# An audio tower's Mamba loop on one Trainium2 core: the order of each engine's work in a loop step is redrawn

## What is computed

```python
h = tok(x)                                   # (64, 128, 256)
xz = layernorm(h) @ W_in                     # 256 -> 2 x 512
xc = silu(conv4(x_inner) + conv_b)           # causal, along the positions
delta_raw, Bm, Cm = split(xc @ W_xproj)      # 1, 16, 16 columns
delta = softplus(delta_raw * w_dt + b_dt)
state = exp(delta * A) * state + delta * Bm * xc      # 16 states for each of 512 channels
y = (sum over states of state * Cm + xc * D) * silu(z)
h = h + y @ W_out
h = h + moe(layernorm(h))                    # softmax, top 2 of 8, silu(x@wg) * (x@wi) @ wo
```

## Time and profile before

| | |
|---|---|
| median of 3 runs | 3155.86 us (3154.88 to 3156.69) |
| profiled execution, its own time | 3151.46 us |
| its span | 3149.5 us |
| busy: PE, DVE, ACT, POOL | 85%, 69%, 47%, 55% |
| Mamba loop (first scan of step 0 to first idle after step 15) | about 120 to 2290 us |
| tail and table, then experts | 2290 to 2341 us, then to the end |
| mean granted TensorE clock | 0.94 of 2.4 GHz |

### The profile page before, as it was taken

The page is one execution under the profiler, slowest core; times in us unless marked ns, Lnnn a source line. Parts: engine busy times, 40 slices in busy tenths (PEclk is TensorE's granted clock), DMA queues, the critical chain, the costliest instruction groups (busy, mean ns, idle before and its releaser), DMA issues. The chain is left out here.

```text
span 3149.5 us, 32678 instructions
## 1 busy us (share of the span) xinstructions
PE 2668.0 (85%) x7774; PEld 1311.5 (42%) x7775; DVE 2170.9 (69%) x2417; ACT 1475.8 (47%) x2717; POOL 1722.5 (55%) x816
## 2 busy tenths in 40 slices
PE   3588897887978788797878879788659999999999
PEld 1234343333434333343433334343236666666665
DVE  0499898988989889898988989899932222222222
ACT  1565556466565646655564665556312222222222
POOL 1467667576766757676675767667522222222222
PEclk9899898999989899998989998898879999999999
DMA  1321304132140413213040321303152222222221
GB/s 37 122 84 50 135 13 140 41 113 104 42 137 10 140 40 114 104 42 135 12 140 30 123 104 42 134 11 136 36 194 45 46 42 45 43 45 45 43 46 30
DMA packets 125600, 235.91 MB, mean 75 GB/s; under 512 B 46449, under 2 KB 93714, under 8 KB 109122
## 3 DMA queue, kind: packets, MB, share of 16 engines
q1 hardware_dynamic: 99378, 200.65, 19.3%
q0 software_dynamic: 26128, 34.36, 6.3%
HBM read 182.22 MB, written 53.78 MB: 75 GB/s over the span
## 5 line engine op out<-in xcount | busy, mean ns | idle before, releaser
L531 POOL TENSOR_TENSOR arena<-u,arena 128x2048 f32<-128x2048 f32 x256 | 1158.3, 4527 | 468.8 <-DVE psum L898 464.0
L1216 PE MATMUL psum<-hc,ident 128*128 128x512 f32 x2048 | 1094.9, 662 | 340.2 <-DVE hc L906 339.5
L898 DVE TENSOR_TENSOR_SCAN psum<-psum,arena 128x1024 f32<-128x1024 f32 x512 | 1172.4, 2290 | 135.7 <-ACT psum L709 112.4
L1216 PEld LDWEIGHTS psum<-hc,ident 128*128 128x128 f32 x2048 | 390.4, 205 | 893.7 <-DVE hc L906 546.5
L709 ACT ACTIVATE psum<-delta,a_neg 128x508 f32<-128x508 f32 x1024 | 656.5, 674 | 0.6
L906 DVE TENSOR_TENSOR hc<-psum,arena 128x1024 f32<-128x1024 f32 x512 | 626.2, 1223 | 15.5
L595 POOL DMA_INDIRECT out_dram<-hres,tok_id x136 | 211.6, 1556 | 598.6 <-ACT hres L835 549.5
L1348 PE MATMUL psum<-arena,xnt 128*128 x1088 | 515.6, 596 | 0.0
L1108 DVE COPY z<-psum 128x512 f32<-128x512 f32 x136 | 94.1, 692 | 461.3 <-PE psum L1357 461.3
L835 ACT ACTIVATE hres<-psum,tok_w 128x256 f32<-128x256 f32 x136 | 64.5, 474 | 454.4 <-PE psum L1367 447.7
L1367 PE MATMUL psum<-arena,z 128*128 x1088 | 257.1, 379 | 0.9 <-DVE z L1108 0.9
(11 more groups left out here) (147 smaller groups left out, 1961.8 us busy)
## 6 DMA issues: line engine op xcount, KB each, us to landing
arena<-ssm_rows SPq DMA_DIRECT2D x128, 1024.0 KB, 6.1
delta<-expert_rows SPq DMA_DIRECT2D x136, 129.0 KB, 2.1
h_saved_rows<-hnew SPq DMA_DIRECT2D x16, 512.0 KB, 6.6
hres<-h_saved_rows SPq DMA_DIRECT2D x16, 512.0 KB, 4.2
out_dram<-h SPq DMA_DIRECT2D x16, 512.0 KB, 3.0
draw<-ssm_rows SPq DMA_DIRECT2D x16, 256.0 KB, 4.0
arena<-in_L_ffn_wg_dram SPq DMA_DIRECT2D x8, 512.0 KB, 9.9
arena<-in_L_ffn_wi_dram SPq DMA_DIRECT2D x8, 512.0 KB, 10.0
```

What stands on the lines that cost most here:

```text
L531: pool.tensor_tensor(dBx[k % 2], rep, b_rep[:, q * QN:(q + 1) * QN, :], ALU.mult).then_inc(dbx_ready, 1)
L898: nc.vector.tensor_tensor_scan(h, h, src, 0.0, ALU.mult, ALU.add).then_inc(scan_done, 1)
L1216: last = nc.tensor.matmul(yacc, ident[:, :], hc[k % 2][:, i, :], start=False, stop=(k % HC == HC - 1 and i == 1))
```

## The change

Nothing is computed otherwise; places in the lists move, and two buffers with them.

- VectorE: `gate_y` of a chunk stands one half unit later (k = 9, 17, 25, and 1 of the next step, before: 8, 16, 24, 0). `residual` at 6 and 8 (5 and 9), `stats2` at 10 (9), `stats1` at 18 (30), `router_a` at 26 (19), `router_b` cut in three at 27, 28, 29 (all at 21), `router_c` at 31 (24).
- TensorE: `project_z` at 0 to 3 (0, 1, 4, 5), `project_out` at 4 to 7 (2, 3, 6, 7), `turn_xn` at 6, 7 (8, 9), `project_x` and `conv` from 8 to 19 (10 to 21), `x_ssm` at 21 (23), `turn_x` at 12, 13 and `embed` at 14, 15 (25 to 28), `turn_row` at 23, 24 (15, 16), `router` at 25 (18), `count` at 30 (22). `skip` stays at 0, 8, 16, 24.
- ScalarE: its copies follow these; `norm1` at 4 (3), `silu_x` at 20 (22), `norm2` at 21, 22 (12, 13), softplus at 25 to 29 and 31 (26 to 29 and 31).
- GpSimd: both sets of scatters of group g - 2 in step g, in units 2, 3, 6, 7 (before: the first set in step g - 1, units 13, 14; the second in step g, units 1, 2); `rsqrt` for the second normalization in unit 8 (6); that for the first, now of group g + 2, in unit 11 (1). Those of group 1 come before the loop.
- SyncE: `save_h` ahead of `share_ssm`.
- `xt` lies in `yz` and no longer in `h2`; both results of `embed` use `bank_b`.

```diff
-        xt = [h2[0:KX, 2 * m:2 * m + 2, :].rearrange("p b c -> p (b c)") for m in range(2)]
+        xt = [yz[0:KX, 2 + m, :] for m in range(2)]
-        emb_bank = [bank_a, bank_b]
+        emb_bank = [bank_b, bank_b]
 # SyncE, step
+                if more:
+                    save_h(g + 2)
                 if not last:
                     share_ssm(g + 1)
-                if more:
-                    save_h(g + 2)
...
 # GpSimd, step and tail
+                    if not second:
+                        if k in (2, 3):
+                            scatter(g - 2, 0, 2 * (k - 2))
+                        if k == 5:
+                            second_weight(g - 2)
+                        if k in (6, 7):
+                            scatter(g - 2, 1, 2 * (k - 6))
+                    if k == 8 and not first:
                         rsqrt(g - 1, 1, stat2, pow2)
+                    if k == 11 and more:
+                        rsqrt(g + 2, 0, stat1, pow1)
...
+            def tail(g):
+                both_scatters(g - 1)
+                rsqrt(g, 1, stat2, pow2)
+                both_scatters(g)
...
 # ScalarE, step (its new places)
+                    if k < NCH:
+                        evac_z(g, k)
+                        if k == 4:
+                            norm1(g + 1)
+                        if k in (6, 7):
+                            evac_xnt(g + 1, k - 6)
+                        if k in (8, 11, 14, 17):
+                            evac_xi(g + 1, (k - 8) // 3)
                         if k in (10, 13, 16, 19):
+                            evac_conv(g + 1, 1 - par, (k - 10) // 3)
+                        if k == 20:
+                            silu_x(g + 1, 1 - par)
...
 # VectorE, step
-                    if k == 0 and not first:
+                    if k == 1 and not first:
                         gate_y(g - 1, NCH - 1)
-                    if k > 0 and k % HC == 0:
+                    if k > 1 and k % HC == 1:
                         gate_y(g, k // HC - 1)
                     times_c(g, k)
...
 # TensorE, step
-                    if k in (0, 1, 4, 5):
-                        project_z(g, {0: 0, 1: 1, 4: 2, 5: 3}[k], not last)
-                    if k in (2, 3, 6, 7) and not first:
-                        project_out(g - 1, k // 4, k % 2, more)
+                    if k < NCH:
+                        project_z(g, k)
+                    if k in (4, 5, 6, 7) and not first:
+                        project_out(g - 1, (k - 4) // 2, k % 2)
                     if not last:
+                        if k in (6, 7):
+                            turn_xn(g + 1, k - 6)
+                        if k in (8, 11, 14, 17):
+                            project_x(g + 1, (k - 8) // 3)
+                        if k in (9, 12, 15, 18):
+                            conv(g + 1, (k - 9) // 3, 0)
                         if k in (10, 13, 16, 19):
+                            conv(g + 1, (k - 10) // 3, 1)
+                        if k == 21:
                             x_ssm(g + 1, 1 - par)
+                    if more:
+                        if k in (12, 13):
+                            turn_x(g + 2, k - 12)
+                        if k in (14, 15):
+                            embed(g + 2, k - 14)
                     if not first:
+                        if k in (23, 24):
+                            turn_row(g - 1, k - 23, more)
+                        if k == 25:
                             router(g - 1)
+                        if k == 30:
                             count(g - 1)
```

More of the change, by code:

```diff
@@ L561, in step, with both_scatters @@
                         make_u(g, par, c)
[L562 to L568, removed]
-                        rsqrt(g - 1, 1, stat2, pow2)
[L570 to L577, removed]
+                    if not second:
[6 more added lines that the diff above has]
+                    if k == 8 and not first:
+                        rsqrt(g - 1, 1, stat2, pow2)
+                    if k == 11 and more:
+                        rsqrt(g + 2, 0, stat1, pow1)
+            def both_scatters(g):
                 scatter(g, 0, 0)
@@ L788, in step @@
[L788 to L798, removed]
@@ L799, in step @@
-                    if k == 29 and not last:
-                        softplus_relu(g + 1, 1)
-                        softplus_relu(g + 1, 2)
+                        if k == 25:
+                            softplus_abs(g + 1)
+                        if k == 26:
+                            softplus_exp(g + 1)
+                        if k == 27:
+                            softplus_ln(g + 1)
+                            softplus_relu(g + 1, 0)
+                        if k in (28, 29):
+                            softplus_relu(g + 1, k - 27)
@@ L938, in router_a, with router_b @@
                 nc.vector.tensor_tensor(ex[:, :, :], logits, bc(lmax[:, :]), ALU.subtract).then_inc(lsub_ready, 1)
-            def router_b(g):
-                dve.wait_ge(lexp_ready, g + 1)
-                nc.vector.tensor_reduce(esum[:, :], r_ex, AX_X, ALU.add).then_inc(dv, 1)
-                after(g, 2)
-                nc.vector.reciprocal(einv[:, :], esum[:, :]).then_inc(dv, 1)
-                after(g, 3)
-                nc.vector.tensor_tensor(r_gates, r_ex, bc(einv[:, :]), ALU.mult).then_inc(dv, 1)
-                n = 4
-                ahead(dve, second_set, g)
-                for k, src in ((0, r_gates), (1, r_g2)):
+            def router_b(g, part):
+                if part == 0:
+                    dve.wait_ge(lexp_ready, g + 1)
+                    nc.vector.tensor_reduce(esum[:, :], r_ex, AX_X, ALU.add).then_inc(dv, 1)
+                    after(g, 2)
+                    nc.vector.reciprocal(einv[:, :], esum[:, :]).then_inc(dv, 1)
+                    after(g, 3)
+                    nc.vector.tensor_tensor(r_gates, r_ex, bc(einv[:, :]), ALU.mult).then_inc(dv, 1)
+                    ahead(dve, second_set, g)
+                if part in (1, 2):
+                    k, src, n = ((0, r_gates, 4), (1, r_g2, 10))[part - 1]
                     after(g, n)
@@ L1045, in tail @@
                 router_a(g)
-                router_b(g)
+                for part in range(3):
+                    router_b(g, part)
                 router_c(g)
@@ L1141, in turn_x @@
                     ahead(pe, emb_free, 2 * g)
-                    ahead(pe, slot_ready, g - 2)
+                    ahead(pe, h2_ready, 2 * (g - 2))
                 else:
@@ L1323, in tail @@
                     for b in range(2):
-                        project_out(g, m, b, False)
-                turn_row(g, 0)
-                turn_row(g, 1)
+                        project_out(g, m, b)
+                turn_row(g, 0, False)
+                turn_row(g, 1, False)
                 router(g)
```

113 lines of the change are left out of this document (43 added, 70 removed).

## The result

The changed kernel takes 3239.69 us (median of 4 runs, 3237.93 to 3242.37) against 3155.37 us (4 runs, 3152.49 to 3156.69): ratio 1.0268, 95% interval 1.0253 to 1.0283, 84 us slower. The direction was forecast; the time lies 18 us above the top of the range. The profiled execution has a span of 3236.8 us at a mean granted clock of 0.938, against 3149.5 and 0.939: the clock as a whole has not changed. One of the four runs of the kernel of experiment 3 took 6392.02 us, the others 3103.68 to 3111.43; its ratio is of those three, as fast runs are compared only with fast ones.

What follows compares the result with a forecast made beforehand. VectorE was taken to bound the loop. New waits of 15.1 against 13.5 us a step give +19, edges +4, tail +2: +25 on 3151.46, 3176, plus 4.4 for the median, 3181 us; range 3132 to 3222.

Steps and rivals of the forecast that it cites:

- What is removed: VectorE's waits for ScalarE and for TensorE ahead of gates: all 161.8 us, 13.5 a step, taken as gone.
- The wait that the change adds: Late skip delays TensorE, ScalarE's copies and the scans: 9.7 us a step, 15.1 with the clock's 5.4.
- Third gap: TensorE idle 4.0 us ahead of skip at half unit 24: 1.8 us for low clock, almost sure.
- Second gap: TensorE idle 3.2 us ahead of skip at half unit 8: 1.8 us for low clock.
- First gap: TensorE idle 0 to 4.4 us ahead of skip at half unit 0: 1.8 us for low clock, least sure.
- that rival's 3235: Rival that all three clock gaps are paid in full, 3.3 us each, waits 19.6 a step: 3235 us; chance 0.17.
- What of VectorE's time is no wait stays: VectorE's time per step apart from waits stays at 137.7 - 13.5 = 124.2 us.
- All this at nothing: GpSimd's scatters and rsqrt, SyncE's transfers, and the moved xt and embed buffers add no time.
- steps 1 to 5: Five places along one full step, from scan 3 to router_a: waits of 2.2, 2.3, 2.6, 2.3 and 0.3 us.
- The tail: After the loop, GpSimd's scatters pass the last statistics by 2 us, between 0 and 5: +2 us.
- No change: Rival: waits of 12.5 to 13.5 us a step, 3149.6 to 3162 us; chance 0.11.
- gaps cost little: Rival: one short clock dip a step, waits 11.4 us, 2.1 a step less, 3137 us; chance 0.25.

Runs made afterwards that it cites:

- experiment 3: Changed kernel with the gates alone put back to half units 0, 8, 16, 24: 3111.08 us, ratio 0.9852.
- experiment 9: Two separate runs on the changed kernel with the three edits: first residual at half unit 5, not 6, 3044.96 us; embedding at 20 and 22, not 14 and 15, 3048.36 us.
- experiment 1: Changed kernel with router_c at half unit 30 instead of 31: 3207.62 us, ratio 1.0171.
- the changed kernel with the three edits: Changed kernel with gates back at half units 0, 8, 16, 24, router_c at 30 and a reduction in place of the copy: 3063.54 us, ratio 0.9714.
- the last kernel: The changed kernel with the three edits, plus first residual at half unit 5 and embedding at 20 and 22: 3034.42 us, ratio 0.9618.
- experiment 6: Kernel before with the gates alone moved to half units 1, 9, 17, 25: 3197.27 us, ratio 1.0134.
- experiment 5: Changed kernel with dummy matmuls ahead of skip at half unit 24: two 3233.95 us, ratio 1.0249; four 3223.11 us, ratio 1.0216.
- experiment 2: Changed kernel with a reduction over an axis of length one in place of the copy into row: 3217.54 us, ratio 1.021.
- experiment 4: Changed kernel, gates late, with TensorE's other pieces of the next half unit ahead of skip at 0, 8, 16, 24: 3147.7 us, ratio 0.9978.

## Why the prediction was right and where it failed

The direction and the waits of the full steps came as forecast. The time did not, because of four terms: VectorE's own work and the jump back, which I had put at nothing, and the steps at the edges and the tail, which I had put too low.

**What is removed: right for the gates, too generous as a whole.** Of the 161.8 us the 67.6 are gone. The 3.60 us ahead of scan 30 are gone too: no scan from 27 to 31 has a wait of any size in steps 2 to 13. But I counted as gone the 0.8 us a step at scan 0 (1.9 in five of twelve steps), and that is where the jump back lies.

**The wait that the change adds: right in place and in sum.** Forecast 15.1 us a step, measured 14.3 (171.6 over 12). The first number of the forecast is the wait at full clock, the second what I put on it for the clock:

| | forecast | measured |
|---|---|---|
| half unit 2 and scan 3 | 2.2 + 1.8 | 4.05 (1.61 and 2.44) |
| scan 8 | 2.3 | 2.44 |
| half unit 10 and scans 12 to 17 | 2.6 + 1.8 | 3.53 (0.59 and 2.94) |
| scan 22 | 2.3 | 2.42 |
| half unit 26 and `router_a` | 0.3 + 1.8 | 1.83 (1.40 and 0.43) |

Experiment 3 shows that the first and the last line hang on the late gate, experiment 9 that scan 8 does not: it is late through the residual. Scan 22 does not hang on the gate alone either: with the gates early it waits 0.5 us, and 2.4 again once the embedding stands at 20 and 22.

**The clock: the size came out about right, the places did not.** What the table has above my waits at full clock is 1.85 + 0.9 + 1.53 = 4.3 us a step, for 5.4 forecast and 9.9 as the upper bound. The rows bear this out to different degrees:

- Third gap: shown. Four dummy matmuls took away the 1.83 us for which I had put 0.3 + 1.8.
- Second gap: shown within the trace. It is 3.10 us in all twelve steps. In seven of them `skip` and `add_state` ran at full clock, half unit 10 did not wait and scan 12 waited 0.3 us; in the other five they were slow and the waits were 1.1 to 2.3 and 0.7 to 0.9 us. That makes some 0.75 us a step, less than half of my 1.8.
- First gap: no run has it at full clock, so its 1.85 is only the difference from my own 2.2. I had called it the least sure; it slowed `skip` or `add_state` in all twelve steps, and in the five at the jump it was 7.7 to 8.3 us long.

So that the sum came near 5.4 is in part luck. The Trainium skill (TensorE: Matmul & The Clock Gate, section HAM oscillation — how this bites in real kernels) says that a gap in the matmuls that recurs in a loop throttles the clock anew on every pass; the trace agrees for the gaps at 0 and 24, where the clock fell in all twelve steps, and not for that at 8, where it fell in five. The full price, 9.9 us a step, did not come. The measured time lies within 5 us of that rival's 3235, but not for its reason: its waits would have been 19.6 us a step.

**"What of VectorE's time is no wait stays": this step failed.** I took 124.2 us as fixed. The copy takes 1.9 us more in each of steps 1 to 14 (2.04 for 0.16), and steps 2 to 13 are 20.5 us longer in busy time. I had looked for what the moved small operations are worth as cover, and not for what runs beside them in their new place.

**"All this at nothing": failed for the jump.** Not in the list of what I costed is that `router_c` at 31 is now the last thing ahead of the jump back to the head of the loop, which comes after every second step. It took 25.0 us in five places where 1.9 each had stood (9.4 in all), so against the kernel before it adds 15.6; experiment 1 gave back 15.

**The sum by its terms**, against the 87.3 us by which the spans differ:

| | forecast | measured |
|---|---|---|
| steps 2 to 13, waits of steps 1 to 5 and those removed | +19 | +10 |
| jump back | 0 | +25 |
| VectorE busy longer | 0 | +20.5 |
| steps 2 to 13, not assigned | | +1.5 |
| from the start to step 2, step 14, step 15 | +4 | +20.6 |
| tail | +2 | +10.5 |
| experts | 0 | -0.8 |

The +10 of the first line are 171.6 less the 161.8 of before, and the first three lines with the 1.5 make the 57.0. The span thus grew by 62 us more than forecast: the copy, the jump, the edges and the tail are too low in my sum, the waits of the full steps 9 too high. The edges were mis-sized in kind: I gave them +1 us each, since they have fewer pieces. They have the same late gates. Step 14 waits 14.1 us in all, for 8.4 before, and has the copy besides; step 1 waits 14.5 for 12.0 and has it too, step 0 waits 14.5 for 9.4 (its start left out). Of the waits that the change removes they had less to lose.

**The tail** was mis-sized by 8.5 us. My bounds were 0 and 5 us for the statistics being passed by the scatters; they were passed by 10.4, for two reasons that I had before me: the landing, which I named and did not price (4.80), and GpSimd's stall in front of its second scatter. That stall stood in the kernel before too (5.91 us at a scatter at 2270.92), under cover of the last step. In the changed kernel with the three edits it is 7.09, in the last kernel 6.89, in that of experiment 6 only 3.30. What releases it was not tried, and stays open.

**The rivals.** "No change" and "gaps cost little" are out by the time, and experiment 5 shows a gap that costs. But what the second says of the rest of the change is true: without the late gates, the jump and the copy, the order wins 92 us.

## What to carry to other kernels

A wait of the engine that sets the pace is paid once; moving it to an engine without slack, here TensorE ahead of the late `skip`, makes it wait too, lose its clock and hand the delay on through the copies to the next scans, so first ask whether the wait needs moving: three of four gates hardly waited once the projections came first, and even in the old order the late gate cost 42 us. When small operations move, read the other engines' rows at the new place: what GpSimd does in those microseconds, and what is last before a jump back. And price the edges and the tail by their own rows, since a stall without a releaser costs nothing where it is covered and all of itself where the cover ends.

## What the runs showed of the hardware that I had not expected

- A copy of 128x4 on VectorE beside a multiplication of GpSimd takes 2.04 to 2.13 us and ends with it (the changed kernel, steps 1 to 14), behind it 0.16 (the kernel before); a reduction that writes the same takes 0.15 beside it (experiment 2).
- After its last small operation VectorE stands some 5 us over the jump back (4.6 to 5.5 in the six kernels with `router_c` at 31, with no releaser); where a scan and a product stand behind the last small operation, only 1.8 to 2.2 show, which the profile puts down to ScalarE. The Trainium skill (Runtime: NRT & Kernel Launch, section Instruction fetch mechanics) says that a taken branch to code that isn't loaded makes the engine fetch it before it goes on. By that rule the trace agrees, in that the stall stands only where the loop jumps and not between the two steps of one pass; that it is the fetch no run here shows.
- At half unit 24, at the end of a stretch in which TensorE had little but `add_state`, a gap of 2.11 us was followed by a low clock (0.57 over the next 2 us) in the kernel with two dummy matmuls, and one of 1.2 us in that of experiment 4; with four dummy matmuls and 0.40 us it stayed up. A gap of 3.10 us at half unit 8, behind a full stretch, was followed by full clock in seven of twelve steps.
- GpSimd stands 5.9 to 7.2 us without a releaser ahead of a scatter near the end of the loop, in all kernels but that of experiment 6 (3.3 us).
